# Two transformer layers with experts on one core: the last pass's experts are held in SBUF and copied into the ring, and the state recurrence runs over 1024 tokens

## What is computed

```python
# layer 0 attention: per channel, over the tokens
y = (e1 * aa + e2 * v) / (e1 * bb + e2); aa, bb = decayed sums of exp(k) * v, exp(k)
x = x + ga * ((sigmoid(r) * y) @ W_out.T)
# layer 1 attention: 16 heads of 8; S is 8 x 8 per head
y_t = r_t @ (S + u * k_t v_t);  S = d_t * S + k_t v_t
x = x + ga * ((head_norm(y) * silu(g)) @ Wo.T)
# both layers: 8 experts of width 512, each token goes to its best 2
out[t] = sum over 2 experts e: gate[t, e] * (act(h[t] @ W1[e] (+ b1[e])) @ W2[e] (+ b2[e]))
```

## Time and profile before

| what | us |
|---|---|
| median of three executions | 601.23 (600.13 to 606.91) |
| profiled execution, whole | 602.57 |
| its span, first to last instruction | 600.7 |
| TensorE busy | 481.6 (80%) |
| VectorE busy | 299.4 (50%) |
| ScalarE busy | 218.9 (36%) |
| POOL busy | 197.8 (33%) |

### The profile page before, as it was taken

How to read it: one execution, slowest core, us unless ns; L and a number is a source line. 1 busy time by engine, 2 the same in 40 slices (tenths; PEclk the granted TensorE clock), 3 DMA queues, 4 the chain that set the end, 5 groups by cost and what they waited for, 6 DMA issues and landing times. The chain is left out here.

```text
span 600.7 us, 8204 instructions
## 1 busy us (share of the span) xinstructions
PE 481.6 (80%) x2744; PEld 376.5 (63%) x2744; DVE 299.4 (50%) x618; ACT 218.9 (36%) x486; POOL 197.8 (33%) x201
## 2 busy tenths in 40 slices
PE   6933995777995899999996879989999857694961
PEld 3721794775995673487784745367779746593960
DVE  2498799200433145588955477469874471000001
ACT  3142414625581433752442131653234311132430
POOL 1000007753337463032231003565432204456340
PEclk9575997878997797999999666999999955677895
DMA  8000016364557453044402012535654034656534
GB/s 261 1 1 0 2 40 230 121 142 161 170 183 252 129 149 88 1 157 142 127 9 72 0 35 84 175 97 156 176 159 126 9 106 159 201 160 177 168 113 140
DMA packets 35241, 70.29 MB, mean 117 GB/s; under 512 B 6162, under 2 KB 19206, under 8 KB 35200
## 3 DMA queue, kind: packets, MB, share of 16 engines
q1 hardware_dynamic: 25152, 57.43, 30.1%
q0 software_dynamic: 5888, 10.25, 7.2%
q10 hardware_dynamic: 4160, 2.10, 1.2%
HBM read 62.40 MB, written 9.18 MB: 119 GB/s over the span
## 5 line engine op out<-in xcount | busy, mean ns | idle before, releaser
L466 POOL DMA_INDIRECT xg<-h_rows,source x92 | 95.9, 1042 | 203.8 <-DVE source L1290 150.9
L475 POOL DMA_INDIRECT y_rows<-ys,dest x92 | 98.4, 1070 | 173.6 <-ACT ys L605 155.3
L857 PE MATMUL PP<-w_ring,hid 128*128 128x128 f32 x736 | 105.2, 291 | 27.4 <-ACT hid L596 20.3
L857 PEld LDWEIGHTS PP<-w_ring,hid 128*128 128x128 f32 x736 | 95.9, 202 | 36.0 <-issue 31.0
L842 PE MATMUL PP<-xs,w_ring 128*128 128x128 f32 x736 | 104.9, 297 | 4.0 <-issue 2.4
L842 PEld LDWEIGHTS PP<-xs,w_ring 128*128 128x128 f32 x736 | 99.3, 212 | 11.0 <-issue 8.6
L605 ACT ACTIVATE ys<-PP,slot_gate 128x128 f32<-128x128 f32 x92 | 34.1, 372 | 96.3 <-PE PP L857 70.6
L592 ACT ACTIVATE hid<-PP,b1q 128x128 f32<-128x128 f32 x184 | 51.3, 379 | 29.9 <-PE PP L842 21.7
L1302 DVE TENSOR_TENSOR arena<-arena 128x512 f32<-128x512 f32 x8 | 5.5, 690 | 106.9 <-DMA arena<-y_rows 95.9
L596 ACT ACTIVATE hid<-PP 128x512 f32<-128x512 f32 x46 | 27.3, 597 | 55.0 <-PE PP L842 27.6
L974 PE MATMUL PP<-arena,consts 128*128 128x512 f32 x64 | 33.7, 611 | 0.8 <-DVE arena L1362 0.5
(11 more groups left out here) (193 smaller groups left out, 706.5 us busy)
## 6 DMA issues: line engine op xcount, KB each, us to landing
w_ring<-experts_dram SPq DMA_DIRECT2D x92, 512.0 KB
arena<-y_rows SPq DMA_DIRECT2D x16, 256.0 KB
h_rows<-htok ACTq DMA_DIRECT2D x4, 512.0 KB
xg<-h_rows,source POOLq DMA_INDIRECT x92
y_rows<-ys,dest POOLq DMA_INDIRECT x92
x<-x_t_dram SPq DMA_DIRECT2D x4, 256.0 KB, 5.3
out_t_dram<-x SPq DMA_DIRECT2D x4, 256.0 KB, 3.5
H<-wmod_dram SPq DMA_DIRECT2D x2, 384.0 KB, 6.2
```

What stands on the lines that cost most here:

```text
L466: pool.indirect_dma_start(xg[:, n % XG, :], None, h_rows[h], bass.IndirectOffsetOnAxis(source[:, h % 2, q:q + 1], 0)).then_inc(s_xg[n % XG ...
L475: pool.indirect_dma_start(y_rows[h], bass.IndirectOffsetOnAxis(dest[:, h % 2, q:q + 1], 0), ys[:, n % YR, :], None, bounds_check=TOPK * T ...
L857: last = pe.matmul(ps, hid[:, n % HID, c * P:(c + 1) * P], w_ring[:, n % WR, FH + c * P:FH + (c + 1) * P], start=(c == 0 and h >= NB), sto ...
```

## The change

**Weights of pass 3.** `experts_home` loads the eight experts of layer 1 once, 4 MB, into `home`, a part of the arena that is the projections' working space of batch 1 and the K and R tiles: six experts behind the load of block 12 of pass 2, when all projections are done, two behind its last load, when both state loops are done. For pass 3 SP loads nothing into the ring; instead `copied` on VectorE reads each block's expert into a register and copies its 128x1024 weights from `home` into the ring's slot. `first_w` no longer holds the loads of blocks 2 and up back until the first rows are turned.

**State loop.** A step now covers 1024 tokens: the spread goes to two banks at once, one VectorE instruction multiplies both, one scan runs over all of them, `carry` is gone. `woven` and `chained` go, too.

**Banks.** A block has one bank for both stages, of `FS` = 3, instead of two for each stage. So stage 1 waits until the block three earlier is weighted, and stage 2 for all four parts of `hid`. To free banks, R of layer 0's batch 1 is copied out of PSUM first and its sigmoid is taken in SBUF.

**Order.** All four rows of `ORDER` are new.

```diff
-XG, WR, YR, HID = 8, 6, 8, 2
+XG, WR, YR, HID, FS = 8, 6, 8, 2, 3
-WARM = 72
+WARM = 71
 ORDER = {
-        "g23 s23 g23 s23 g20 s5 g3 s18 g12 s2 g4 s g7 s20",
+        "g11 s g3 s3 g5 s2 g4 s7 g3 s2 g s2 g3 s3 g2 s2 g s g6 s g5 s g2 s21 g20 s3 g3 s20 g22 s2 g s21",
...
             def first_w(h):
                 sp.wait_ge(s_expert, h + 1)
                 for q in range(WR):
-                    if q == 2 and h != 1:
-                        sp.wait_ge(s_xt, NQ * h + 1)
                     load_w(h, q)
+            def experts_home(a, b):
+                sp.dma_start(home[:, a:b, :], wp_d[NE + a:NE + b].rearrange("e p n -> p e n")).then_inc(s_home, 16)
             for h in range(HALVES):
-                for q in range(WR, NQ):
-                    load_w(h, q)
+                if h < HALVES - 1:
+                    for q in range(WR, NQ):
+                        load_w(h, q)
+                        if h == HALVES - 2 and q == 2 * WR:
+                            sp.wait_ge(s_mx, BPB * len(JOBS) * NB)
+                            sp.wait_ge(s_mxa, BPB * NACT * NB)
+                            sp.wait_ge(s_mxd, BPB * NDVE * NB)
+                            experts_home(0, NLATE)
+                if h == HALVES - 2:
+                    sp.wait_ge(s_prod, HK * NB)
+                    experts_home(NLATE, NE)
...
             def stage1(h, q):
-                pe.wait_ge(s_w[n % WR], 16 * (n // WR + 1))
+                if h < HALVES - 1:
+                    pe.wait_ge(s_w[n % WR], 16 * (n // WR + 1))
+                else:
+                    pe.wait_ge(s_copied, q + 1)
-                if n >= 2:
-                    pe.wait_ge(s_hid, NC * (n - 1))
+                if n >= FS:
+                    pe.wait_ge(s_ys, n - FS + 1)
             def stage2(h, q):
-                if n >= 2:
-                    pe.wait_ge(s_ys, n - 1)
-                ps = PP[:, 2 + n % 2, 0:P]
+                ps = block_bank(n)[:, 0:P]
+                pe.wait_ge(s_hid, NC * (n + 1))
...
+            def copied(h):
+                for q in range(NQ):
+                    yield
+                    n = NQ * h + q
+                    if q == 0:
+                        dve.wait_ge(s_home, 16 * 2)
+                        dve.wait_ge(s_expert, h + 1)
+                    dve.wait_ge(s_p2, n - WR + 1)
+                    e = dve.value_load(expert[0:1, h % 2, q:q + 1], min_val=NE, max_val=2 * NE - 1)
+                    dve.tensor_copy(w_ring[:, n % WR, :], home[:, bass.ds(e - NE, 1), :].rearrange("p e n -> p (e n)")).then_inc(s_copied, 1)
...
-                    dve.tensor_tensor(kv[n % 2], blk(A["K"], i), spread_bank(j), ALU.mult).then_inc(s_kv, 1)
+                    dve.tensor_tensor(kv, A["K"], spread_pair, ALU.mult).then_inc(s_kv, 1)
+                    dve.tensor_tensor_scan(S[n % 2][:, 1:T + 1], A["dec"], kv, 0.0, ALU.mult, ALU.add).then_inc(s_S, 1)
+                    dve.tensor_tensor(prod[n % 2], A["R"], S[n % 2][:, 0:T], ALU.mult).then_inc(s_prod, 1)
```

More of the change, by code:

```diff
@@ L108, in merged @@
         run(parts)
-def woven(*stages):
-    due = [[next(parts), parts] for parts in stages]
-    while due:
-        first = min(due, key=lambda d: d[0])
-        yield first[0]
-        first[0] = next(first[1], None)
-        if first[0] is None:
-            due.remove(first)
-def chained(stages):
-    for parts in stages:
-        yield from parts
 def program(nc, x_d, wrvk_d, wout0_d, cols_d, wmod_d, wp_d, b1_d, b2_d, br_d, wr_d,
@@ L181, in program @@
         headmean = sb("headmean", [P, P // HK])
-        carry = sb("carry", [P, HK])
         upto = sb("upto", [P, P])
@@ L984, in sums @@
-                def sums(i):
-                    for j in range(HK):
-                        yield (ST_BLOCK * i + ST_GATHER + j)
-                        gather(i, j)
+                    else:
+                        pe.wait_ge(s_kv, n)
+                    for i in range(BPB):
+                        pe.matmul(spread_bank(i), sel[:, j, :], blk(v_lo, i), start=True, stop=False)
+                        last = pe.matmul(spread_bank(i), sel[:, j, :], blk(v_hi, i), start=False, stop=True)
+                    last.then_inc(s_vb, 1)
@@ L993, in attn1_state @@
                     pe.wait_ge(s_idx, 3)
-                yield from woven(chained(inputs(i) for i in range(BPB)), chained(sums(i) for i in range(BPB)))
+                bonus()
+                for j in range(HK):
+                    yield
+                    spread(j)
+                    if j >= 2:
+                        yield
+                        gather(j - 2)
+                for j in (HK - 2, HK - 1):
+                    yield
+                    gather(j)
             def group_norm(b):
```

194 lines of the change are left out of this document (95 added, 99 removed), and 23 rows, old and new, of the table ORDER.

## The result

The changed kernel takes **586.25 us** (median of four executions, 584.04 to 588.84) against 602.25 (600.13 to 606.91) for the kernel before: a ratio of **0.973, 95% interval 0.969 to 0.978**. I had forecast 570, with a range of 556 to 587. The sign and the range hold, but the gain is 16 us instead of 31, about half.

The account below looks back on a forecast made before the run. The last pass was taken as bound by transfers and POOL's queue order, earlier passes mostly by TensorE. Terms -20 (last pass), -8 (hand-over), -4 (loops), +1 (loading) gave -31 us: a median near 570 us, range 556 to 587.

Parts of the forecast that it names:

- The last pass is bound by transfers: Pass 3, 84 us with 59.5 busy on TensorE, was said to wait for weight transfers and POOL's queue order.
- Last pass -20: Pass 3 with weights from SBUF: a gain of 20 us, with 11.5 and 27.5 as ends.
- lock-out of POOL: In pass 3 VectorE's copies hold up POOL's indirect DMAs: 8 us taken; as full lock-out rival 578 us, chance 0.10.
- Hand-over -8: From pass 0 to pass 1, new orders let TensorE work while it waited: -8 us, ends 0 and -14.
- the work that now fits there is 9 us: At the hand-over from pass 0 to 1, 80 more TensorE instructions fit into its waiting, 9 us.
- State loops and what follows -4: Both state loops over 1024 tokens: some 8 us per batch saved on VectorE, -4 us in all, ends -12 and +3.
- TensorE is full in these loops: In the state loops TensorE keeps the same matmuls, so VectorE's saving isn't given back where TensorE ends last.
- Loading +1: Loading the eight experts during pass 2 delays the loads behind it: +1 us, 12 us if uncovered.
- Three banks at nothing: One bank of three per block for both stages costs nothing, since other blocks' products cover the gelus.
- the bank rule as rival: Banks held 7.5 us slow every block to 2.5 us: 618 us, slower than before, chance 0.06.
- my point of 20 us more: The forecast is wrong if TensorE's waits for `ys` or `hid` grow by more than 20 us.
- the rival in which the hand-over and the loops give nothing: Only the last pass gains: 580 us; chance 0.17, shared with a ring starved by the load of home.

Follow-up runs that it names:

- third run: The kernel before the change, with only the eight experts loaded into SBUF and copied into the ring in pass 3; 599.63 us, ratio 0.993.
- seventh run: The changed kernel, with TensorE taking the token sums of pass 0 earlier, behind fewer products of pass 1; 586.88 us, ratio 0.970.
- fifth run: The changed kernel repeated without any edit, as the mark for other runs; 583.94 us, ratio 0.966.
- twelfth run: The changed kernel, with VectorE doing each of its three instructions of a state step in two halves of 512 tokens; 596.35 us, ratio 0.971.
- sixth run: The changed kernel, with POOL's order of gathers and scatters in pass 3 as before the change; 586.48 us, ratio 0.969.
- eighth run: The changed kernel, with POOL's gathers of blocks 10 and up in pass 1 spread among the scatters; 578.28 us, ratio 0.946.

## Why the prediction was right in sign and half off in size

- **"The last pass is bound by transfers" failed.** I read it from 157 to 173 GB/s and from chain pieces named "another core or an unknown queue". Home in the kernel before takes 2.1 us off pass 3, in the changed one 5.6 (by single profiles). A high DMA share says that transfers run, not that anyone waits for them, and those pieces say only that the releaser wasn't found: in pass 3 of the changed kernel one still stands in the chain, with no weights on the way (start us, us, what; the group of waits would have told: 19.5 us for `hid`, none for the weights):

```profile
544.40 4.20 another core or an unknown queue
```

- **Last pass -20: measured -13.0**, 5.6 from home and 7.4 from what else changed, the order and the banks, which I had costed at nothing there. The copies are 711 ns as forecast (0.70), and their lock-out of POOL costs 2.6 us on POOL and none on the end, not 8. The rule of the Trainium skill (SBUF — State Buffer, "SBUF: two separate sides") that I weighed allowed up to 18.7 us, an estimate with that page's figure; the trace doesn't show such a price, since all 46 indirect DMAs together are 2.6 us longer. Two terms are mis-sized. TensorE is idle for 71.6 - 53.9 = 17.7 us, 14 more than the 3.5 us before the first product, where I had 2 to 3 us of waits and 8 of contention. And its work took 53.9 us, not 50.
- **Hand-over -8: measured a loss.** A grew by 8.5 us (4.4 against the third run) although loop 0 in it became 7.0 shorter. The first token sum came 12.5 us later, not within 5. My step "the work that now fits there is 9 us" counted what stands in the queue; from 183 to 203 us TensorE did 97 instructions instead of 62, but it is idle there for 8.6 us where it was for 9.4. What the step left out is POOL's order: spreading its long run of gathers in pass 1, and nothing else, takes TensorE's idle time in A from 44.2 to 33.8 us and A to 235.1, 10.3 us less. By which waits it does so isn't shown. The token sums as such don't matter (seventh run).
- **State loops and what follows -4: B measured -11.8 or -3.7, by the clock.** The steps take 4.66 us as forecast (4.6) and each loop is 7 us shorter, near the 8 that I had for VectorE. B splits into 7.0 us of loop 1, 3.9 before and 0.9 behind it, but this doesn't show that all of the 7.0 us reach the end. TensorE did 229 instructions in loop 1 instead of 269, and behind it 325 instead of 290 in the same 44.2 us of busy time, at a clock of 0.88 instead of 0.81. Its idle time in B, which the clock doesn't touch directly, fell by 3.5 us (19.1 to 15.5), and by 4.4 in the fifth run (14.7), whose B at the clock of before is 3.7 us shorter. That is the -4 of the forecast: "TensorE is full in these loops" held in its result, though a loop itself follows VectorE. Of loop 0, the twelfth run shows little in A (246.5 against 245.9 with a loop 3.2 us longer).
- **Loading +1: measured 0** (B and loop 1 are the same to 0.1 us with and without it).
- **Three banks at nothing, the bank rule as rival:** TensorE waits 11.6 us for `ys` and 18.9 for `hid` in the whole run, against 23.2 for `hid` in the second stage before; my point of 20 us more isn't reached. 71.6 us for pass 3 lies just in the forecast 60 to 72 (73.9 in the repeat doesn't); "the unknown queue vanishes from its chain" didn't hold.

The account: passes 0 to 2 were forecast at -8 - 4 + 1 = -11 and gave +8.5 - 11.8 = -3.3, the last pass gave -13.0 instead of -20, the start and the tail -2.2: -18.5 in place of -31. That the time still fell inside the range owes something to luck: 8.1 of the 11.8 us in B are a granted clock that the fifth run's profile of the same program doesn't have, and outside pass 3 I had put nothing down to the clock, while TensorE's busy time is 17.0 of the 18.5 us.

One sum of the prediction slipped: the rival in which the hand-over and the loops give nothing should add 8 + 4 us, which gives 582, not 8 + 2. No chance or bound hangs on it.

## What to carry to other kernels

Before a transfer is removed, look for a wait that names it; a busy DMA and an unnamed piece of the chain are no evidence, and the cheapest test is to take the transfer away alone. A serial loop follows the engine whose instructions depend on each other, even where another engine is always busy; but the kernel gains only as far as that other's work finds idle time elsewhere (loop 1 lost 7.0 us, TensorE's idle time in B some 4). Before a gain is put down to the change, compare TensorE's busy time and granted clock for the same instructions in both profiles, and profile the same kernel twice. Where one queue mixes gathers and scatters, try short runs while other engines exchange short steps (10 us here, but only 3 to 4 with a still finer order), but not where the gathers themselves are only just ahead (7 us lost in pass 3).

## What the runs showed that I had not expected

- **Long runs of indirect DMAs and late releases.** In passes 0 and 1 ScalarE goes on only 1.4 to 2.1 us after a run of POOL's ends, up to 9 us behind the end that TensorE's rows give; SP's load that waits for the same products as the gelu of 202.75 us is issued at 203.39. The waits repeat in five profiles (7.48 to 7.50 us; the other one 12.44 to 12.51), but not in all: with the same POOL order the first is 3.31 us in the sixth run, and the second is 8.4 or 7.0 us or absent in the sixth, seventh and twelfth. What couples POOL to them isn't shown. TensorE's ends in a profile are modelled, so the products may really have ended late: counted from the first gather, the sixth run's rows end them 3.4 us later than the first profile's, while ScalarE and SP go on at the same time to 0.6 us.
- **The clock decides 8 us by chance.** With the same instructions, and TensorE busy for 18.3 and 19.4 of 20 us at the projections, B is 161.8 or 169.9 us, and the granted clock in these 20 us is 0.83 or 0.50.
- The kernel of the eighth run beats both: 0.946 of the time before, 2% below the changed kernel by the ratios and 1% by the medians, by an order of POOL in pass 1 alone.
